# Segment sums of the last five edge chunks as identity products on TensorE, tail weights and raw rows moved around them

## What is computed

```python
xn = _layernorm(x)
out1 = segment_sum(edge_attr, dst, n)
out2 = segment_max(edge_attr, dst, n)         # 0 where a node has no edge
out3 = out1 / maximum(count, 1)
h = concatenate([xn, out1, out2, out3, u[batch]], axis=1)
gnn = relu(h @ W1 + b1) @ W2 + b2 + xn
mix = (v + q2 @ (k2.T @ v) / sqrt(N)) @ W_out + b_out   # k2, q2: normalised squares of keys, queries
x = x + gnn + mix
x = x + feed_forward(layernorm(x))            # of the 3124 nodes with the largest weights
```

## Time and profile before

| | |
|---|---|
| median of 3 runs | 1189.91 us (1189.75 to 1193.56) |
| profiled execution | 1188.52 us |
| its span | 1186.8 us |
| busy: TensorE matmul, VectorE, ScalarE, GpSimd | 1014.9, 1009.5, 500.0, 463.2 us |
| end of the edge stage | 502.1 us |
| node loop, selection, feed-forward | from 525 us |

### The profile page before, as it was taken

One profiled execution on the slowest core, in us unless ns is written; L12 is line 12 of the kernel. 1 busy time (PEld: TensorE's weight loads), 2 busy tenths in 40 slices (PEclk: granted clock), 3 DMA queues, 4 the chain that ended last, 5 costly groups with the idle time before them and its releaser, 6 DMA issues.

```text
span 1186.8 us, 15897 instructions
## 1 busy us (share of the span) xinstructions
PE 1014.9 (86%) x4571; PEld 762.3 (64%) x4571; DVE 1009.5 (85%) x2424; ACT 500.0 (42%) x1487; POOL 463.2 (39%) x344
## 2 busy tenths in 40 slices
PE   2387889999977568078999999999999995899996
PEld 1254555656634445057888888888888982488886
DVE  7899999999999999967988889888897868576574
ACT  3657666778832244332322333223332333243341
POOL 0088840888400000476654446644443000223331
PEclk9699998999996879569999999999999996599999
DMA  9699999999988999732433324433243130111110
GB/s 347 255 328 363 361 358 339 358 367 378 338 300 321 408 397 379 257 93 67 156 125 127 127 88 155 133 127 129 78 137 109 57 115 19 37 36 42 45 43 20
DMA packets 94927, 234.97 MB, mean 198 GB/s; under 512 B 13089, under 2 KB 67654, under 8 KB 88594
## 3 DMA queue, kind: packets, MB, share of 16 engines
q1 hardware_dynamic: 50450, 157.00, 35.6%
q10 hardware_dynamic: 30192, 43.66, 10.3%
q0 software_dynamic: 14224, 33.61, 10.0%
HBM read 153.68 MB, written 80.55 MB: 197 GB/s over the span
## 4 chain that ended last, share of the span: by engine, by line
PE 49%; DVE 3%; POOL 2%; issue 1%; DMA 0%; ACT 0%; DVEq 0%; POOLq 0%
PE psR L67 5%; PE psC L67 5%; PE psQ L56 5%; PE psQ L57 5%; PE psQ L58 5%; PE psKx L56 5%; PE psKx L57 5%; PE psKx L58 4%; PE psR L68 3%; PE psC L68 2%; PE psT L2126 1%; PE psQ L2147 1%; PE psKx L2147 1%; POOL graw L468 1%; PE psR L66 1%
## 5 line engine op out<-in xcount | busy, mean ns | idle before, releaser
L468 POOL DMA_INDIRECT graw<-in_edge_attr,ic x98 | 141.3, 1441 | 76.3 <-DVE ob L1001 40.7
L998 DVE SCALAR_TENSOR_TENSOR ob<-ob,mQ,mx 128x96 f32<-128x96 f32 x392 | 122.8, 313 | 4.4
L1001 DVE SCALAR_TENSOR_TENSOR ob<-ob,kQ,xb 128x96 f32<-128x96 f32 x392 | 122.5, 312 | 0.1
L677 POOL DMA_INDIRECT near<-ends_d,blki x49 | 87.7, 1790 | 71.5 <-DVEq L906 56.9
L677 POOL DMA_INDIRECT near<-in_dst,rowi x49 | 87.8, 1792 | 59.7 <-DVEq L915 45.1
L1795 ACT ACTIVATE hT_hi<-psQ 128x512 fp32r<-128x512 f32 (+2 forms) x52 | 29.8, 573 | 185.5 <-PE psQ L2147 185.5
L1935 PE MATMUL psQ<-Wqk,xT 128*128 128x512 f32 (+1 forms) x196 | 95.5, 611 | 0.0
L986 DVE TENSOR_TENSOR xb<-xb 128x1536 f32<-128x1536 f32 x49 | 86.1, 1758 | 1.7
L984 DVE TENSOR_TENSOR mx<-xb 128x1536 f32<-128x1536 f32 x49 | 85.6, 1747 | 1.2 <-DVE carry L1056 0.2
L67 PE MATMUL psR<-W2w,hT_hi 128*128 128x512 f32 x175 | 65.7, 411 | 3.8 <-DVE x L1164 3.8
L1795 ACT ACTIVATE hT_hi<-psKx 128x512 fp32r<-128x512 f32 (+2 forms) x52 | 29.8, 573 | 90.9 <-PE psKx L2147 90.9
(11 more groups left out here) (523 smaller groups left out, 3237.5 us busy)
## 6 DMA issues: line engine op xcount, KB each, us to landing
xb<-in_edge_attr SPq DMA_DIRECT2D x49, 1536.0 KB, 10.4
scan_d<-ob SPq DMA_DIRECT2D x49, 768.0 KB, 6.0
yrow_d<-yr SPq DMA_DIRECT2D x48, 132.0 KB
xg<-in_x ACTq DMA_DIRECT2D x12, 512.0 KB, 11.9
xT_d<-xT ACTq DMA_DIRECT2D x12, 512.0 KB, 8.1
base_d<-dcur ACTq DMA_DIRECT2D x12, 512.0 KB
qT_d<-qT ACTq DMA_DIRECT2D x12, 512.0 KB, 9.8
out_x<-xres SPq DMA_DIRECT2D x48, 128.0 KB
```

Source lines behind the costliest of these rows:

```text
L468: nc.gpsimd.indirect_dma_start(out=to.rearrange("p i f -> p (i f)"), out_offset=None, in_=raw_v, in_offset=bass.IndirectOffsetOnAxis(ap=ic ...
L677: nc.gpsimd.indirect_dma_start(out=near[:, t, :], out_offset=None, in_=table, in_offset=bass.IndirectOffsetOnAxis(ap=rows[:, t:t + 1], axi ...
L998: nc.vector.scalar_tensor_tensor(o[:, q, 0:EF], prev[:, 0:EF], mQ[:, bass.ds(c * TQ + q, 1)], mx[:, q, 0, :], ALU.min, ALU.max).then_inc(s ...
L1001: nc.vector.scalar_tensor_tensor(o[:, q, EF:AGG], prev[:, EF:AGG], kQ[:, bass.ds(c * TQ + q, 1)], X[:, q, 0, :], ALU.mult, ALU.add).then_i ...
```

## The change

For chunks 44 to 48 the two sum instructions on VectorE go. `quad_sums` lets TensorE add the four edges of each quad instead: identity times rows i = 0 to 3, accumulated in `psR` for quads 0 to 3 and in `psC` for 4 to 7; the scan step reads there. Chunk 44's stand inside the attention (before the weight work of group 10), those of 45 to 48 behind it, each half behind the scan steps that read the bank before. The tail parts go behind the carried products, on ScalarE behind the masked rows. The raw rows of group 0 get a place of their own, `raw0`, over the space for base and attention rows, whose loads in turn go behind `masked_rows`. Weights are loaded three chunks earlier, segment ends, gather rows and masks worked out two earlier. At the start VectorE does the node statistics before the bias row. In the passage group 0's aggregates no longer stand behind the wait for the tail weights.

```diff
+SUMS = (44, 45, 46, 47, 48)
...
+            raw0 = nc.alloc_sbuf_tensor_at("raw0", [P, GT, 8, EF], f32, offset=at[0] - 4 * GT * NF * 4)
...
+            psS = [psR, psC]
...
-                    if c == 39:
+                    if c == 36:
 
                         sp.wait_ge(s_at, 6 + KF)
                         sp.wait_ge(s_fs, TILES)
-                    if c in (39, 40):
-                        for i in range(2 * (c - 39), 2 * (c - 39) + 2):
+                    if c in (36, 37):
+                        for i in range(2 * (c - 36), 2 * (c - 36) + 2):
...
-                early(0, s_g0r)
+
+                pool.wait_ge(s_t2, TILES)
+                for e in range(4):
+                    pool.wait_ge(s_t2o[e], 16 * (GROUPS // 4 + (e == 0)))
+                gather_raw(0, GT, P, s_g0, raw0)
...
+                    on_pe = c in SUMS
+                    n0 = sum(2 if k in SUMS else 4 for k in range(c))
                     dve.wait_ge(s_load[b], g * 16 + 16)
                     nc.vector.tensor_tensor(mx[:, :, :, :], xp[:, :, :, 0, :], xp[:, :, :, 1, :], ALU.max).then_inc(s_tree, 1)
-                    dve.wait_ge(s_tree, c * 4 + 1)
-                    nc.vector.tensor_tensor(xp[:, :, :, 0, :], xp[:, :, :, 0, :], xp[:, :, :, 1, :], ALU.add).then_inc(s_tree, 1)
+                    dve.wait_ge(s_tree, n0 + 1)
+                    if not on_pe:
+                        nc.vector.tensor_tensor(xp[:, :, :, 0, :], xp[:, :, :, 0, :], xp[:, :, :, 1, :], ALU.add).then_inc(s_tree, 1)
...
+                        if on_pe and q % 4 == 0:
+
+                            dve.wait_ge(s_pt, 4 + SUMS.index(c) * 2 + q // 4 + 1)
+                        quad_sum = psS[q // 4][:, q % 4 * EF:(q % 4 + 1) * EF] if on_pe else X[:, q, 0, :]
...
-                                                       X[:, q, 0, :], ALU.mult, ALU.add).then_inc(s_sum, 1)
+                                                       quad_sum, ALU.mult, ALU.add).then_inc(s_sum, 1)
...
-                bias_row()
                 for g in range(4, GROUPS + 1):
                     stats(g)
+                variances()
+                bias_row()
                 query_bias()
-                variances()
                 deviations()
...
-                    dve.wait_ge(s_wlo, LOWS + 4)
-                    nc.vector.memset(yr[:, :, NF:YROW], 0.0).then_inc(s_u, 1)
-                    dve.wait_ge(s_u, 1)
                     for part in range(3, 5):
                         aggregate(0, 0, 0, part)
                     repair()
+                    dve.wait_ge(s_wlo, LOWS + 4)
+                    nc.vector.memset(yr[:, :, NF:YROW], 0.0).then_inc(s_u, 1)
+                    dve.wait_ge(s_u, 1)
...
+                def quad_sums(c):
+
+                    pe.wait_ge(s_load[c % XB], c // XB * 16 + 16)
+                    for h in range(2):
+                        if c != SUMS[0]:
+
+                            pe.wait_ge(s_sum, (c - 1) * TQ + 4 * h + 5)
+                        for i in range(4):
+                            ins = nc.tensor.matmul(psS[h][:, 0:4 * EF], ident[:, :], xb[c % XB][:, 4 * h:4 * h + 4, i, :],
+                                                   start=(i == 0), stop=(i == 3))
+                        ins.then_inc(s_pt, 1)
...
+                    if g == 10:
+                        quad_sums(SUMS[0])
                     weights(g)
                 attention(GROUPS, 0, GROUPS // 4 * 16 + 16)
-                for i in range(4):
-                    tail_part(i)
-
+
+                pe.wait_ge(s_t2, TILES)
                 pe.wait_ge(s_lead, 1)
-                nc.tensor.matmul(psR[:, :], ones[:, :], endrow[:, :], start=True, stop=True).then_inc(s_t, 1)
+                nc.tensor.matmul(psT[0][:, :], ones[:, :], endrow[:, :], start=True, stop=True).then_inc(s_t, 1)
+                for c in SUMS[1:]:
+                    quad_sums(c)
```

More of the change, by code:

```diff
@@ L482, in wait_chosen @@
                 if g == 0:
-                    engine.wait_ge(s_g0[t], 16)
+                    engine.wait_ge(s_g0[t], 32 + 16)
                 elif t == 0:
@@ L1060, in _ @@
                         dve.wait_ge(s_t, 2)
-                        step(nc.vector.tensor_scalar(leads[:, :], psR[:, :], fixf[:, 0:1], None, ALU.is_equal))
+                        step(nc.vector.tensor_scalar(leads[:, :], psT[0][:, :], fixf[:, 0:1], None, ALU.is_equal))
                 dve.wait_ge(s_t, 3)
@@ L1248, in node_stage @@
                     carries()
+                    for part in range(3, 5):
+                        aggregate(0, 0, 0, part)
+                    repair()
                     dve.wait_ge(s_wlo, LOWS + 4)
@@ L1251, in node_stage @@
                     dve.wait_ge(s_u, 1)
-                    for part in range(3, 5):
-                        aggregate(0, 0, 0, part)
-                    repair()
                     for t in range(GT):
@@ L1737, in _ @@
                 act.dma_start(xTr[0][:, :, :], xT_d[0:1, :, :, :].rearrange("o p c n -> p (o c) n")).then_inc(s_ld[0], 16)
-                weights(GROUPS)
                 for e in range(4):
@@ L1747, in _ @@
                         act.dma_start(to[:, :, :], src[e * GT * P:(e + 1) * GT * P, :].rearrange("(t p) f -> p t f", p=P)).then_inc(s_lb[e], 16)
[L1749 to L1765 removed]
+                weights(GROUPS)
                 def node_stage():
@@ L2110, in _ @@
                 ins.then_inc(s_t, 1)
+                for i in range(4):
+                    tail_part(i)
                 def node_stage():
```

69 lines of the change are left out of this document (34 added, 35 removed).

## The result

The changed kernel took **1198.77 us** (median of 13 runs, 1185.31 to 1204.99) against 1190.81 us for the kernel before beside it: a ratio of 1.0056 [1.0036, 1.0076], **slower** by more than the interval, where 1176 and faster was forecast. The profiled execution took 1202.75 us (span 1201.0).

A forecast was written before the change was run, and what follows sets the result against it. VectorE bounds the scan, then short waits, then TensorE in the node loop. Terms -12.7 + 1.2 + 4.3 - 5.5 - 1.5 = -14.2 us against 1188.52 give 1174.3, as median 1176 us; range 1170.5 to 1179, to 1184 with rivals 1, 3 and 4.

The forecast's parts named there:

- the attention's end: TensorE's attention, ending at 467.3 us before, was to end at 454, from 28.9 MB moved at 400 GB/s after 382.
- the term of +1.2 us for chunk 45's sums: In the scan, chunk 45's sums would come late on TensorE after a fallen clock; nothing if straight from the attention.
- tail products in the passage, +4.3: On TensorE between scan and node loop: tail products put edge products 27.2 us behind the scan's end, not 22.9.
- Five chunks lose their sums: VectorE, chunks 44 to 48: 2.54 us less per chunk, 6.5 us each, -12.7 us in all.
- rival 4: Scan steps reading PSUM beside TensorE's writes take 0.05 us more in 40 steps: 2 us, 1178; chance 0.05.
- rival 1: DMA queues hold the attention at its old end, TensorE reaches chunk 45 at 468: +8.5 instead of +1.2, 1183; chance 0.15.
- Chunk 44's sums stand inside the attention and nobody waits for them: TensorE's sums for chunk 44, 5.2 us of work, would cause no wait.
- The start: Node statistics before the bias row bring VectorE's next step to 46.7 from 48.27: -1.5 us, between 0 and -3.0.
- Raw rows: Fetched early; masks end 2.2 us behind the scan's end, first aggregate 3.8; gathered scan rows may hold it 1 or 2.
- E: The end of VectorE's scan, 502.1 us in the profile before; later times are given as E plus something.
- The hole: TensorE's 3.78 us wait for GpSimd's sum in the node loop and 1.7 us of half clock go: -5.5 us.
- rival 2: TensorE at 1.2 GHz through sums (+15.6), then behind the scan (+11.6): 1202, chance 0.07; if swinging, 1189, chance 0.04.

The follow-up runs named there:

- the run after: The changed kernel's first profiled execution, nothing else edited: 1202.75 us, against 1188.52 us for the profiled kernel before.
- the six traces: Six profiled executions of the changed kernel, nothing edited: 1202.75, 1186.59, 1195.62, 1201.42, 1200.73 and 1193.98 us.
- again: The changed kernel once more, nothing edited: median 1187.65 us, ratio 1.0005 to the kernel before; profiled execution 1186.59 us.
- again_e: The changed kernel once more on a further chip, nothing edited: 1191.09 us, ratio 1.0031 to the kernel before; profiled execution 1193.98 us.
- no_sums: The changed kernel with no sums on TensorE, all chunks' sums back on VectorE: 1199.05 us, ratio 1.0042 to the kernel before.
- sums_46: The changed kernel with sums on TensorE for chunks 46, 47 and 48 alone: 1192.87 us, ratio 1.0026 to the kernel before.
- skip_45: The changed kernel with chunk 45's sums alone back on VectorE: 1191.04 us, ratio 1.0004 to the kernel before.
- adds_early: The changed kernel with GpSimd's two sums of base and attention rows ahead of its group 2 gathers: 1192.32 us, ratio 1.0031 to the kernel before.
- adds_out: The changed kernel with nearly all of GpSimd's two sums for the first two node groups left out: 1195.63 us, ratio 1.0057 to the kernel before.
- again_c: The changed kernel once more, nothing edited: 1201.42 us, ratio 1.0113 to the kernel before.
- three_late: Changed kernel, TensorE sums for chunks 46 to 48 only, tail parts behind 46's, ScalarE's last copies before late transfers: 1180.81 us, 0.9928; another chip 1178.96, 0.9922.

## Why the prediction was wrong

**The step that failed first is the attention's end, forecast at 454 and measured at 472.1, which made the term of +1.2 us for chunk 45's sums one of +9.8. The term for the tail products in the passage, +4.3, failed in a part of the executions. The rivals that name the two had too small a chance.**

1. *Five chunks lose their sums.* The size was right: 6.50 us a chunk, and no added time for scan steps from PSUM (rival 4 did not happen). What failed is that it pays five times. Three pay; chunk 44 and 45 wait 9.8 us between them in the run after (8.7 to 14.4 in the six traces), where I counted 1.2.

2. *"From 382 us to the attention's end go six chunks of 2.36 MB ... thus 454."* **This is the step that failed first**, and it is enough to fix the scan's end, which stands 27.5 us behind the start of chunk 45's sums in all six traces. In 72 us eight chunks of 9.05 us pass, not six, so my own count was inconsistent. From 380 to 472 us the run after issues 9 loads and 9 dumps: 9 x 2.36 + 3.8 + 11.0 = 36.0 MB, and 35.76 MB moved, at 389 GB/s. The DMA view, 382 to 454 us, before and after:

```profile
DMA packets 9094, 28.23 MB, mean 392 GB/s; under 512 B 567, under 2 KB 5736, under 8 KB 8197
```

```profile
DMA packets 9298, 28.23 MB, mean 392 GB/s; under 512 B 622, under 2 KB 5862, under 8 KB 8447
```

The same 28.23 MB at the same 392 GB/s: the queues were full before and moved no more. The 13.5 us that ScalarE had waited for weights were taken back by the transfers that it issues, two of which held it for over 8 us:

```profile
405.41 8.73 ACTq L1687 DMA_DIRECT2D qT<-qT_d  x1
414.18 1.05 ACT L1711 CAST W1f_hi<-rW 128x1024 fp32r<-128x1024 f32 x1 [9.26 <-issue]
...
433.90 8.44 ACTq L1687 DMA_DIRECT2D kc<-qT_d  x1
```

"Attention rows could have moved in the 13.5 us in which ScalarE stood still, and did not" was therefore no argument against rival 1. Rival 1 happened: it had +8.5 in place of +1.2, and +9.8 was measured. Without chunk 44's sums the attention ended at 462.3 to 467.2, so 0 to 5 us ahead of its old end of 467.4 and not 13. That the queues are the reason rests on these rows; no run lightened them.

3. *"Chunk 44's sums stand inside the attention and nobody waits for them."* Wrong: VectorE waited 2.8 us for them, and the attention ended later with them than without, 470.6 against 465.2 in the middle of the traces; the sums take 5.2 us.

4. *The start.* Chunk 1 came 0.85 us earlier in the run after instead of 1.5, in `again` not at all, and 0.5 to 1.2 us earlier in the other four. Nothing of it reaches the scan's end, which TensorE sets.

5. *Raw rows.* The masks ended at E + 3.3 (forecast 2.2), but VectorE then waited 5.3 us, 515.37 - 501.2 = E + 14.2, for gathered scan rows, which hang on E:

```profile
515.37 0.56 DVE L1121 TENSOR_TENSOR kept<-kept,grow 128x384 f32<-128x384 f32 x1 [5.27 <-issue]
```

I had given them "1 or 2 us". TensorE came later anyway here, so it changed nothing.

6. *Tail products in the passage, +4.3.* Right for one kind of execution only: E + 26.5 in `again` and 25.9 in again_e against 27.2. The hole, forecast to give 5.5 us, gave 3.9 in `again` and 1.3 in again_e. The working let the clock rise after 2 us. In five of the eleven traces in which the tail products stand where the change puts them (six of the changed kernel itself, no_sums, sums_46, skip_45, adds_early, adds_out) it stayed at 1.2 GHz to the end of the tail products, and rival 2's second half, to which I gave 0.07 and 0.04 together with its first half, is a mechanism; the collision of VectorE and GpSimd, which the prediction doesn't have, adds to it. Its first half did not happen: in all six traces of the changed kernel each half chunk's sums took 2.74 to 2.82 us, the full clock's price.

The prediction weighed the Trainium skill's "TensorE: Matmul & The Clock Gate", section on psum-queue depth-cycling, against rows. Between the groups of sums the clock stayed up in the run after, so the rows were the better guide there; behind E it lay at 1.2 GHz for 27 us with TensorE 69 to 100% busy in stretches of 8 us (again_c), without a swing.

With these terms set right the forecast would have been an E near 500 instead of 489.1, and a time from 1186 in one kind of execution to about 1200 in the other: no change, or slower. What decides between them stays open.

## What to carry to other kernels

Before counting on an engine that is freed from a wait, check whether the DMA queues moved less during that wait than around it; if bytes per microsecond are the same, the wait may reappear as another one, as it did here. Move work only into a place that an engine reaches in time: three sums after the attention paid nearly in full (6.7 to 7.6 us), the two at its end cost more than they saved. A long run of float32 products right behind a stretch with half-idle TensorE may fall wholly into its low clock and cost double; the same products between pieces of work at full clock ran in 7.4 us and held up VectorE by 1.7 us at most (three_late, whose ratios are 0.9922 and 0.9928). And one profile does not show such a spread: take several executions before explaining a small difference.

## What was not expected of the hardware

- One program had executions of 1183.7 and of 1203.6 us on the same chip. In its six traces the clock behind the scan was at 1.2 GHz for 27 us (1200.73 and 1201.42) or for about 7 (1186.59 to 1202.75).
- Issuing a transfer held ScalarE for 8.73 us with the DMA share at 1.04. In the kernel before, issues of the same kind took 0.5 to 1.7 us, though the share reached 1.02 there too; what makes an issue wait was not found.
- A VectorE instruction of 0.55 us took 5.58 beside GpSimd's two float32 sums of 128x1024 (4.70 together).
- Work that TensorE had finished was taken up 2.5 to 8.6 us late by other engines, in traces with fewer records only; this is not explained.
